# ALiBi's distances of the first group's third head group: four TensorE products replaced by four ScalarE writes into the scores' banks

## The reference

```python
q = split(hidden_states @ Wq.T + bq)
k = split(hidden_states @ Wk.T + bk)
v = split(hidden_states @ Wv.T + bv)
scores = jnp.einsum('bhsd,bhtd->bhst', q, k)
rel = (pos[None, :] - pos[:, None]).astype(scores.dtype)
bias = alibi_slopes[:, None, None] * rel
scores = (scores + bias[None]) / math.sqrt(HD)
scores = 30.0 * jnp.tanh(scores / 30.0)
scores = jnp.where(causal[None, None], scores, -jnp.inf)
probs = jax.nn.softmax(scores, axis=-1)
ctx = jnp.einsum('bhst,bhtd->bhsd', probs, v)
return ctx @ Wo.T + bo
```

## Time and profile before

| what | value |
|---|---|
| median of 3 runs | 546.66 us (546.57 to 546.98) |
| the profiled execution, its own time | 546.76 us |
| its span, first to last instruction | 545.0 us |
| PE busy | 538.2 us, 99% of the span |
| DVE, ACT, POOL busy | 375.1, 283.1, 290.3 us (69%, 52%, 53%) |
| granted TensorE clock | 1.00 of full speed in the whole span |
| chain that ended last | PE 82%, POOL 10%, DVE 5%, issue 2% |

### The profile page before, as it was taken

How to read it: one execution, slowest core, us unless ns; L and a number is a source line. 1 busy time by engine, 2 the same in 40 slices (tenths; PEclk the granted TensorE clock), 3 DMA queues, 4 the chain that set the end, 5 groups by cost and what they waited for, 6 DMA issues and landing times.

```text
span 545.0 us, 10146 instructions
## 1 busy us (share of the span) xinstructions
PE 538.2 (99%) x3936; PEld 424.2 (78%) x3936; DVE 375.1 (69%) x717; ACT 283.1 (52%) x510; POOL 290.3 (53%) x262
## 2 busy tenths in 40 slices
PE   8999999999999999999999999999999999999997
PEld 7877888878888888888888888766686667866676
DVE  6999886888665886659898987355944668344422
ACT  5857886977767786776653442034501344023310
POOL 5398798985783657877795348034400343013320
PEclk9999999999999999999999999999999999999999
DMA  8951222273215310239563712100071001600001
GB/s 291 342 212 65 77 81 78 79 228 123 75 44 161 111 59 2 79 109 299 187 238 101 266 32 103 41 1 0 0 155 38 1 0 27 149 20 0 1 20 59
DMA packets 56176, 53.91 MB, mean 99 GB/s; under 512 B 15168, under 2 KB 37952, under 8 KB 56128
## 3 DMA queue, kind: packets, MB, share of 16 engines
q1 hardware_dynamic: 56128, 53.25, 31.0%
HBM read 36.46 MB, written 13.63 MB: 92 GB/s over the span
## 4 chain that ended last, share of the span: by engine, by line
PE 82%; POOL 10%; DVE 5%; issue 2%; ACT 0%; POOLq 0%; DVEq 0%
PE bank L312 33%; PE bank L506 24%; PE bank L526 15%; POOL q_w L828 2%; POOL q_w L826 2%; POOL probs L819 2%; POOL x_res L842 2%; PE bank L307 2%; PE bank L440 2%; PE bank L450 1%; PE bank L409 1%; DVE q_m L1363 1%; PE bank L361 1%; PE bank L537 1%; PE bank L556 1%
## 5 line engine op out<-in xcount | busy, mean ns | idle before, releaser
L312 PE MATMUL bank<-reduced 128*128 128x512 f32 x936 | 223.3, 394 | 0.3 <-DVE ctxT L1307 0.3
L312 PEld LDWEIGHTS bank<-reduced 128*128 128x128 f32 x936 | 172.8, 188 | 38.2 <-issue 1.1
L934 POOL TENSOR_TENSOR f_parts<-fused,f_parts 128x512 fp32r<-128x512 f32 x48 | 62.9, 1310 | 154.3 <-ACT f_parts L1206 154.3
L1188 ACT ACTIVATE tanh_g<-bank,half_gate 128x512 f32<-128x512 f32 x48 | 33.0, 687 | 141.8 <-PE bank L506 133.0
L526 PE MATMUL bank<-reduced,f_parts 128*128 128x512 f32 x360 | 83.5, 392 | 0.0
L526 PEld LDWEIGHTS bank<-reduced,f_parts 128*128 128x128 f32 x360 | 67.4, 188 | 14.2
L506 PE MATMUL bank<-reduced 128*128 128x512 f32 x288 | 72.1, 402 | 0.0
L1552 DVE SCALAR_TENSOR_TENSOR silu<-tanh_g,bank 128x512 f32<-128x512 f32 x48 | 32.9, 685 | 56.8 <-ACT tanh_g L1188 56.8
L506 PEld LDWEIGHTS bank<-reduced 128*128 128x128 f32 x288 | 54.1, 188 | 12.9
L826 POOL TENSOR_TENSOR q_w<-q_w,q_m 128x512 f32<-128x512 f32 x36 | 49.7, 1381 | 7.8 <-DVE q_m L1365 7.8
L819 POOL TENSOR_SCALAR_AFFINE_SELECT probs<-probs 128x1024 f32<-128x1024 f32 x32 | 37.0, 1161 | 31.0 <-ACT probs L1001 31.0
(11 more groups left out here) (135 smaller groups left out, 761.9 us busy)
## 6 DMA issues: line engine op xcount, KB each, us to landing
quantized<-q_w SPq DMA_DIRECT2D x36, 256.0 KB, 3.4
reduced<-quantized SPq DMA_DIRECT2D x12, 512.0 KB, 6.8
memT_sb<-in_memT SPq DMA_DIRECT2D x16, 256.0 KB, 4.9
mem_sb<-in_mem SPq DMA_DIRECT2D x16, 256.0 KB, 5.9
out<-y_sb SPq DMA_DIRECT2D x15, 256.0 KB, 2.1
q_w<-in_gate_w SPq DMA_DIRECT2D x12, 256.0 KB, 3.5
q_w<-in_up_w SPq DMA_DIRECT2D x12, 256.0 KB, 3.2
x_res<-in_x SPq DMA_DIRECT2D x3, 1024.0 KB, 8.9
```

Of the source, the lines that this page charges most:

```text
L312: ins = pe.matmul(dst, stationary, moving, start=(n == 0), stop=(n == len(pairs) - 1))
L934: pool.tensor_tensor(f_lo[:, f, :], fused[:, f % 2, :], f_hi[:, f, :].bitcast(F32), ALU.subtract).then_inc(f_lo_ready, 1)
```

## The change

One entry is added to the table, and the condition that kept group 0 from seeding its third head group is gone. ScalarE's four writes stand after the copy of K of (0, 2) and ahead of `context_high` of (0, 0); TensorE's scores of (0, 2) take the way of `scores_onto`. As (0, 2) is now the first entry, the wait for the distance table stands there too. Nothing else of the program changes.

```diff
-SEEDED = ((1, 1), (1, 2), (2, 2), (3, 2))
+SEEDED = ((0, 2), (1, 1), (1, 2), (2, 2), (3, 2))
...
                 heads(g, 1, 2)
                 q_out(g, 2)
                 k_out(g, 2)
-                if g:
-                    seed(g, 2)
+                seed(g, 2)
                 if g == 0:
                     context_high(g, 0)
                 else:
```

## The result

The changed kernel takes 548.86 us, the median of 5 runs (548.55 to 549.13), beside 546.98 us for the kernel before in the same session (5 runs, 546.57 to 547.12). The ratio is 1.004 with a 95% interval of 1.0029 to 1.0051: slower by 1.9 us. The forecast was 548.5 us, within 547.8 to 549.4, with 0.86 on slower.

The account below looks back on a forecast made before the run. PE is 99% busy, but in the changed step POOL's list sets the pace: 2.46 us of writes less 0.68 returned gives 1.78, covering PE's own 0.49 and the 0.22 gain. 546.76 + 1.78 = 548.54, forecast 548.5 us, range 547.8 to 549.4.

Parts of the forecast that it names:

- The place: At PE's context of (0, 2), POOL's list, held by ACT's `context_high` of (0, 0), sets the pace; PE waits 0.35 us.
- The writes: Four ACT writes ahead of `context_high` of (0, 0) take 2.46 us, moving `low_part` on POOL from 44.87 to 47.33.
- POOL's pieces: POOL's work from `low_part` to the masks gets 0.68 us shorter, since DVE's slab preparations finish before POOL begins.
- Rival A: POOL's work between `low_part` and the masks stays as long as before, giving 549.2 us; chance 0.2.
- PE's next context: PE's context of (0, 2) starts 1.78 us later, at 56.17, behind POOL's masks.
- PE's own wait: Ahead of the scores of (0, 2), PE idles 1.06 us for the fourth ACT write.
- PE's own lateness: Through waiting for the writes alone, PE would be 0.49 us later at the context of (0, 2).
- Rival B: POOL does not hold the context of (0, 2) back; at least PE's 0.49 us remains, 547.25 us; chance 0.04.
- The gain: Dropping the four L398 products from PE's scores of (0, 2) saves 0.22 us, unless PE is waiting anyway soon after.
- No return later: After the step no later wait gives the delay back; every row from 64 us on is 1.8 us later.
- Rival C: PE's later waits on DVE give back at most 1.0 us of the delay, 547.5 us; chance 0.1.
- rival D: PE's clock falls to 1.2 GHz for the projections of (0, 3) after its waits, 553.0 us; chance 0.03.

Follow-up runs that it names:

- the first experiment: The changed kernel with `context_high` of (0, 0) moved ahead of the copy of K of (0, 2), so before the four writes: 547.58 us, ratio 1.0007 to 1.0025.

## Why the prediction was right

*The place.* POOL was named as what sets the pace in this step, held by `context_high`. Moving `context_high` out of the writes' way takes the wait on POOL away; delaying it without any seeding brings the whole loss. Shown both ways.

*The writes*, expected at 2.46 us: 47.03 - 44.58 = 2.45. `low_part` was to start at 47.33 and started at 47.73; less the 0.35 us from before the step, that is 47.38.

*POOL's pieces*, expected to give back 0.68 us: from `low_part` to the masks 7.05 us became 54.09 - 47.73 = 6.36, so 0.69. That DVE is the reason was argued from lengths; holding DVE showed it. Rival A fell: DVE's four shuffles came under the additions, and these took 2.57 us. One reading was not exact: the preparation of 0.42 us at 44.72 was not wholly beside an idle POOL, since L811 began at 44.87. The four of the changed kernel, all done before POOL began, show the length without POOL, 0.41 to 0.43.

*PE's next context*, expected 1.78 us later: 1.81 in the profile, 1.88 in the medians.

*PE's own wait* was the term that was mis-sized: 1.06 us expected, 1.39 measured. It stood on the scores starting 0.02 us behind the last write; they start 0.36 us behind it (44.58 + 2.51 = 47.09 to 47.45). PE's own lateness is 0.75 us by the first experiment, and not 0.49. It did not matter to the sum, since POOL's 1.81 covers both, and PE's wait on POOL came out at 0.93 in place of some 1.3. Rival B, which lived on that lateness, would have been at 547.5 and not at 547.25.

*The gain* of 0.22 us from the products: 0.23 in the profile where it could show, nothing where PE waits anyway.

*No return later*: 2.16 us at the next context, 2.11 at 115.65, 2.2 in the spans. Rival C fell.

*The clock*, rival D at 0.03: it did not happen in the changed kernel, whose two waits of 1.39 and 0.93 us left it at 1.00 in the profile and at 0.999 or 1.000 in the five runs. But it was nearer than the chance said, since it happened in four runs of five with the wait of 1.67 us and in two of five with the waits of 1.30 and 1.73 us. And its price was too high: I had doubled a whole stage of projections, 553.0 us in all, where the fall cost 1.60 us. The sentence that no row had a lower clock behind a wait was true of the kernel before, and was no evidence for waits in the middle of work that are longer than its own there.

## What to carry to other kernels

An engine that is 99% busy can still be led, in one step, by the slowest list of the others; a short wait of it there (0.35 us here) tells where taking work off it gains nothing. Before giving work to an engine that is half idle, look at what stands behind the new place in that engine's order and who waits for it: four writes worth 0.22 us to TensorE cost 2.45 us to a copy that POOL's whole list hung on. Put what others wait for ahead of what can wait.

## What the runs showed of the hardware that I had not expected

- A wait of 1.67 us in the middle of TensorE's work was followed by a fall of its granted clock to 0.50, for between three and four microseconds and at a cost of 1.60 us; the mean clock was 0.996 or 0.997 in four of five runs. With waits of 1.30 and 1.73 us within ten it was so in two of five, with 1.39 and 0.93 us in none of five. Six products on constants in the wait of 1.67 us kept the clock at 1.000 in all five, on another chip. The Trainium skill ("TensorE: Matmul & The Clock Gate", Part 1) has the clock fall after idleness, and these runs agree in that, with shorter idleness than the page warns of.
- Between the end of ScalarE's last write and the start of the product that waits for it lie 0.36 us (0.37 in the experiment with `context_high` first).
- The same slab preparation on DVE takes 0.43 us while POOL is idle and 1.40 beside it, and POOL's two additions 2.57 and 2.92 us, without and with DVE's preparations beside them. So both sides become longer, each by waiting for the other in turn. In the kernel with DVE held, the preparation at 47.08 began 0.05 us ahead of L811 and kept its 0.43 us, while L811 took 1.52 in place of 1.27. The next one, at 47.54, began under L811 and ended at 48.94, 0.29 us behind L811's end at 48.65; in the kernel before it is 46.58 against 46.29, 0.29 again. The Trainium skill ("SBUF — State Buffer", Who interferes with whom) has the later of the two blocked for the whole of the other's instruction, and these rows fit that.
